# Key-by-query products stored by head instead of interleaved, and a score product that reads one column of each head in turn

## The reference, cut to what matters

```
x   = rmsnorm(hidden) * ln_weight                 # (8, 128, 512)
h_q = (x @ w_q.T), h_k = (ctx @ w_k.T), h_v = (ctx @ w_v.T)    # 32 heads of 128
score = einsum('bqhd,bkhd->bhqk', h_q, h_k) + position_bias
score = softmax(where(mask, score, -inf));  score = where(mask, score, 0)
out = einsum('bhqk,bkhd->bqhd', score, h_v) @ w_out.T ;  hidden + out
```

## Time and profile before

| | |
|---|---|
| median of 3 runs | 775.89 us (772.86 to 777.35) |
| the profiled execution's own time | 776.54 us |
| its span, first to last instruction | 774.7 us |
| granted TensorE clock, mean | 0.992 of full |
| PE busy | 735.4 us, 95% |
| PEld busy | 580.2 us, 75% |
| DVE busy | 485.0 us, 63% |
| ACT busy | 399.7 us, 52% |
| HBM read | 142.23 MB |

### The profile page before, as it was taken

How to read it: one execution, slowest core, us unless ns; L and a number is a source line. 1 busy time by engine, 2 the same in 40 slices (tenths; PEclk the granted TensorE clock), 3 DMA queues, 4 the chain that set the end, 5 groups by cost and what they waited for, 6 DMA issues and landing times.

```text
span 774.7 us, 12357 instructions
## 1 busy us (share of the span) xinstructions
PE 735.4 (95%) x4320; PEld 580.2 (75%) x4320; DVE 485.0 (63%) x823; ACT 399.7 (52%) x617; POOL 90.9 (12%) x86
## 2 busy tenths in 40 slices
PE   6999999999988999999999999999999879999993
PEld 4888888888867777777777777777776547887782
DVE  5653467534353678877796575765557737578555
ACT  5433333333345566655676656656666444554452
POOL 2010000090017000000000031000000002204503
PEclk9999999999999999999999999999999999999997
DMA  8463241342626788778887777776775333433541
GB/s 330 130 215 135 83 147 50 114 123 81 230 84 205 242 309 276 264 262 296 308 271 228 223 229 234 241 230 220 224 238 167 106 102 120 161 124 106 194 133 55
DMA packets 60039, 145.09 MB, mean 187 GB/s; under 512 B 6752, under 2 KB 6768, under 8 KB 59344
## 3 DMA queue, kind: packets, MB, share of 16 engines
q1 hardware_dynamic: 58400, 136.73, 54.1%
q0 software_dynamic: 1360, 7.23, 2.4%
q10 hardware_dynamic: 224, 0.39, 0.2%
HBM read 142.23 MB, written 2.10 MB: 186 GB/s over the span
## 4 chain that ended last, share of the span: by engine, by line
PE 78%; DVE 10%; DMA 6%; issue 3%; ACT 2%; POOL 1%; SPq 0%; DVEq 0%; ACTq 0%; POOLq 0%
PE bank L468 24%; PE acc L468 15%; PE bank L640 7%; PE bank L586 7%; PE acc L721 6%; PE bank L699 6%; PE bank L605 6%; PE bank L682 5%; DMA ak<-ax 3%; DVE score L1321 2%; DMA a_raw<-w 1%; DVE score L1329 1%; DVE neg_max L1327 1%; PE bank L500 1%; PE bank L618 1%
## 5 line engine op out<-in xcount | busy, mean ns | idle before, releaser
L468 PE MATMUL bank<-feat_hi,a_hi 128*128 128x512 f32 x352 | 139.5, 396 | 11.2 <-DVE feat_lo L1104 7.5
L468 PE MATMUL bank<-feat_lo,a_hi 128*128 128x512 f32 x352 | 138.1, 392 | 0.0
L1104 DVE TENSOR_TENSOR a_lo<-a_raw,a_hi 128x1024 fp32r<-128x1024 f32 (+1 forms) x45 | 55.7, 1238 | 127.1 <-ACT a_hi L869 121.0
L1321 DVE TENSOR_TENSOR score<-bank,mask_add 128x512 f32<-128x512 f32 x64 | 42.5, 685 | 100.6 <-PE bank L640 100.6
L586 PEld LDWEIGHTS bank<-few_ctx,ak 128*128 128x128 f32 x512 | 62.0, 191 | 47.1 <-issue 36.1
L468 PE MATMUL acc<-b_hi,tile_hi 128*128 128x512 f32 x224 | 88.3, 394 | 2.6 <-issue 1.9
L998 ACT ACTIVATE t_ring<-bank 128x512 f32<-128x512 f32 x64 | 69.8, 1091 | 37.9 <-PE bank L605 37.9
L468 PEld LDWEIGHTS bank<-feat_hi,a_hi 128*128 128x128 f32 x352 | 66.9, 190 | 28.5 <-DVE a_lo L1104 9.1
L468 PE MATMUL acc<-b_hi,tile_lo 128*128 128x512 f32 x224 | 87.9, 392 | 0.0
L605 PEld LDWEIGHTS bank<-k_ring,wq 128*128 128x128 f32 x512 | 65.6, 192 | 25.1 <-issue 20.1
L586 PE MATMUL bank<-few_ctx,ak 128*128 128x128 f32 x512 | 73.6, 287 | 5.1 <-DMA ak<-ax 3.8
(11 more groups left out here) (113 smaller groups left out, 1100.6 us busy)
## 6 DMA issues: line engine op xcount, KB each, us to landing
ak<-ax SPq DMA_DIRECT2D x64, 512.0 KB, 4.3
wq<-wqn SPq DMA_DIRECT2D x64, 256.0 KB, 4.6
wv<-wvh SPq DMA_DIRECT2D x64, 256.0 KB, 3.5
wo<-bx SPq DMA_DIRECT2D x64, 256.0 KB, 4.4
a_raw<-w SPq DMA_DIRECT2D x22, 512.0 KB, 4.1
a_raw<-a SPq DMA_DIRECT2D x21, 512.0 KB, 3.9
b_raw<-b SPq DMA_DIRECT2D x34, 256.0 KB, 2.7
pair<-w SPq DMA_DIRECT2D x24, 352.0 KB, 4.6
```

Source lines behind the costliest of these rows:

```text
L468: mm = pe.matmul(out_ap, w, x, start=start and k == 0, stop=stop and k == len(products) - 1, skip_group_check=True)
L1104: return dve.tensor_tensor(out_ap, whole, high, ALU.subtract)
L1321: dve.tensor_tensor(score[n % GH][:], bank[2][:].rearrange("p (b k) -> p b k", b=HB), mask_add[j][:, half * HB:(half + 1) * HB, :], ALU.ad ...
```

## The change

`t_ring` gets the head as its outermost index. ACT's copy of one head then writes 512 floats side by side, as they lie in the bank. The score product of the running branch keeps its 128 output columns in the order (k h); its moving operand is read with the same order, so that successive columns come from the four heads in turn, C x HB x FEW = 512 floats (2048 bytes) apart, and after four columns the address goes back and on by one float. The other branch (not run here) reads one head of the ring as its stationary operand, now side by side. No instruction is added or removed, no wait is changed.

```diff
@@ tensors
-        t_ring = two("t_ring", [P, C, HB, FEW, GH])
+        t_ring = two("t_ring", [P, GH, C, HB, FEW])
@@ group_scores
                         for c in range(C):
                             mm = pe.matmul(bank[2][:, b * P:(b + 1) * P], xn[half][:, c, b * SEQ:(b + 1) * SEQ],
-                                           t_ring[g % 2][:, c, b, :, :].rearrange("p k h -> p (k h)"), start=False, stop=(c == C - 1),
+                                           t_ring[g % 2][:, :, c, b, :].rearrange("p h k -> p k h"), start=False, stop=(c == C - 1),
                                            skip_group_check=True)
@@ head_scores (branch for many keys)
-                        mm = pe.matmul(bank[2][:, b * P:(b + 1) * P], t_ring[g % 2][:, b, :, :, j].rearrange("p b k -> p (b k)"),
+                        mm = pe.matmul(bank[2][:, b * P:(b + 1) * P], t_ring[g % 2][:, j, b, :, :].rearrange("p b k -> p (b k)"),
                                        k_ring[:, n % RING, b * SEQ:(b + 1) * SEQ], start=False, stop=True, skip_group_check=True)
@@ copy_queries
-                act.activation(t_ring[n // GH % 2][:].rearrange("p c b k h -> p (c b k h)")[:, n % GH:GH * N:GH], bank[0][:],
-                               ACT.Copy).then_inc(t_ok, 1)
+                act.activation(t_ring[n // GH % 2][:, n % GH].rearrange("p c b k -> p (c b k)"), bank[0][:], ACT.Copy).then_inc(t_ok, 1)
```

## The result

| | before | after |
|---|---|---|
| median | 776.36 us (6 runs) | 834.72 us (6 runs) |
| ratio | | 1.075, 95% interval 1.0725 to 1.0776 |
| the profiled execution's own time | 776.54 us | 833.98 us |
| its span | 774.7 us | 832.2 us |

The kernel became 58 us slower. I had forecast 774.8, with a range from 771 to 808; rival B, which I gave 0.17, said 828. The median before stands here over six executions, three more than in the first table.

The account below looks back on a forecast made before the run. The prediction took PE to bound the kernel: 776.54 us, minus 1.65 for the shorter copy, plus 0.5 for the strided read, gave 775.4, or 774.7 from the median. It forecast 774.8, with its own range from 771.8 to 778.5.

Parts of the forecast that it names:

- rival B: Score product matmuls: operand swept twice, the stride halves both sweeps, 111 ns become 222; 828 us in all; chance 0.17.
- What bounds the kernel: From 246 to 600 us PE is idle only 4.06 us, so time added to its matmuls is paid nearly in full.
- The copy's length: ACT's copy of one head into t_ring: 598 ns instead of 1091, 31.6 us less of ACT's time.
- Its worth: Time the shorter t_ring copy saves on the path: 0.76 + 0.49 + 0.4 = 1.65 us.
- near 250 us: Two PE waits, 0.42 and 0.34 us, on ACT copies queued behind t_ring's both go: 0.76 us.
- near 398 us: First transposes into bank 0, which wait for t_ring and start at 398.03: 0.2 us goes.
- The score product: 512 PE matmuls with the strided moving operand: 0 to 5 ns more each, 0 to 2.6 us, 0.5 taken.
- The page: Skill's rule for SBUF reads: two hits on a 16-byte line hide latency, a new line each access is penalised; no price.
- Rival A: Score product matmuls: the stride adds 57 ns to each, 29.2 us; 802 us in all; chance 0.14.
- Rival C: PE's 4.06 us idle in the stage and 2.8 us of earlier waits all due to ACT; 769 us; chance 0.06.
- rival D: Copy into t_ring stays at about 1.09 us, its length not due to the stride; 776.4 us; chance 0.02.
- Same: Whole kernel: a measured time not told from no change, within about 0.5%, 3.9 us; chance 0.62.

Follow-up runs that it names:

- the copy alone: The changed kernel, but with the score product's moving operand read side by side again (from the wrong heads): 775.33 us against 775.95, ratio 0.9989.

## Why the prediction was wrong, step by step

- **What bounds the kernel**: right. PE had 4.06 us of idle time in the stage, and what was added to its matmuls was paid in full.
- **The copy's length**: right, 593 ns (598 said). ACT's busy time fell by 28.6 us and not by 31.6, since its instructions overlap; the copies alone went from 69.8 to 38.0 us. **Its worth**: too high. 1.65 us worked out, 0.6 measured (interval -0.3 to 1.9), so it can't be told from either 0 or 1.65. The traces show where the step was weak: "what is late next in each place is PE itself" is false near 250 us, where DVE's division is late next and leaves 0.1 us of 0.76, and near 398 us, where the `ak` load is late next and leaves nothing of 0.2.
- **The score product**: the step that failed, and it decides the sign. I took 0 to 5 ns an instruction, 0.5 us in the sum, "because PE's pace in plain float32 is already that of a strided read"; it is 110 ns an instruction, 56.3 us. I had two numbers of PE at hand: a single-pass weight load, 140 ns side by side and 197 strided, and a plain float32 one, 192 side by side. I read them as a floor that plain float32 had already paid. The runs show that plain float32 pays the stride on top of its own pace, on the very side from which I took the row: 330 ns. My text had said that a changed pace would mean an error in carrying a weight load's row over to the moving operand. It was not that: both sides of PE behave alike. The error was to carry a row of the one-pass kind over to plain float32, whose only strided rows were those that I didn't have. The text even calls the transposes' row "the same kind of float"; that a load side by side takes 140 ns in one and 192 in the other was the sign that it isn't.
- **The page**: the Trainium skill (Advanced Engine Details and Errata, SBUF Cachelines) asks for at least two hits on a line. I weighed it as a rule against the change and gave it 0.31 with A and B. For plain float32 the runs agree with it: two floats of a line (8 bytes, 114 ns; pairs; a doubled element) are nearly free, one float of a line costs 217 to 226 ns; only two runs in turn, at 136 ns with no two hits in a row, are much cheaper than it lets expect. In the single pass they don't: two hits on a line by pairs, 467 ns, cost as much as one, and two runs in turn, with a new line each time, take 213 ns.
- **Rival A** (57 ns on top of each) falls. **Rival B** had the size right: 222 ns, 828 us; measured 221 ns and 834.72. Its sum took off 3 us of waits and 1.65 for the copy, and neither came: outside its busy time PE has 774.7 - 735.4 = 39.3 us before and 832.2 - 792.3 = 39.9 after. Its mechanism, two sweeps of the columns at a cycle each, isn't shown. Sweeps of the one-pass kind would make 8 bytes dear in plain float32, and they are free there. What PE does in the four cycles stays open. **Rival C** falls with the 775.33 us of the copy alone, **rival D** with its 591 to 593 ns.
- **The chances**: the unknown cost had bounds of 0 and 57 us, and no row stood between them that had the same kind of operand. "Same" at 0.62 rested on one inference. The forecast's own range is also off by 0.4 us: a read of 0 to 2.6 us and 2 us each way give 772.3 to 778.9, not 771.8 to 778.5; nothing hangs on it. And "a contiguous operand is already the easiest to read" was no row: in the single pass two runs in turn are faster, 213 ns for 227.

## What to carry to other kernels

Where PE is the bound, let the engine that has slack do the strided work: here ACT's copy with every fourth float costs 493 ns a head, 2.0 us a group, of slack; the same interleaving in PE's plain float32 operand costs 32 x 0.110 = 3.5 us a group of PE's time. If a plain float32 moving operand must be gathered, take two neighbouring floats of one line at a time, or put the reordering into the output's address in the bank, which was free at a step of 16 bytes. On the stationary side a step of 8 bytes was nearly free too (196 ns for 192); pairs were not run there. A row about an operand read by PE counts only for the same kind of pass; before relying on a "hidden" stride, look for a row with that kind.

## What the runs showed of the hardware that I had not expected

- Plain float32, 128 columns: 111 ns side by side, 172 at 12 bytes, 217 to 226 from 16 bytes on. That is about 4 cycles of 2.4 GHz for each new 16-byte line (4.1 at 16 bytes; 3.2 a column at 12, where three columns of four bring a new line) and never less than 2 a column.
- Several lines in turn: plain float32 nearly keeps two (136 ns, whether 256 or 4096 bytes apart) and not four (221 ns, at 128 and 2048). Float32r, 512 columns, goes from 227 ns to 213 with two runs in turn, faster than side by side, and to 283 with four, though a mere step of 8 bytes takes 447.
- The bank takes columns 16 bytes apart at full pace in plain float32 (112 ns a matmul).
